# First attention: a pair's two early decay halves as one product of 128 columns, issued beside the late product

## What is computed

```python
g = -jax.nn.softplus(x @ Wg.T + bg)                 # (b, t, H), H = 8
lam = jax.nn.softplus(dl + Lparam[None, None])      # level weights
G = jnp.cumsum(g, axis=1)
scores = jnp.einsum('bthd,bshd->bhts', q, k) * scale
logdecay = Gh[:, :, :, None] - Gh[:, :, None, :]    # G[t] - G[s], Gh is G by heads
logdecay = jnp.where(mask[None, None], logdecay, -jnp.inf)
decay = jnp.exp(logdecay)
lamw = jnp.einsum('bthl,tsl->bhts', lam, lvl_oh)    # by the dyadic level of t - s
A = scores * decay * lamw
y = jnp.einsum('bhts,bshd->bthd', A, v)
```

## Time and profile before

| | |
|---|---|
| median of 3 runs | 1531.12 us (1529.8 to 1531.84) |
| profiled execution | 1537.38 us, span 1535.6 us |
| PE busy | 1417.6 us, 92% of the span |
| DVE, ACT, POOL busy | 920.9 (60%), 801.3 (52%), 660.2 us (43%) |
| chain that ended last | PE 68%, POOL 8%, DVE 7%, issue 6%, ACT 5%, DMA 3% |
| mean granted TensorE clock | 0.966 of full speed |

### The profile page before, as it was taken

How to read it: one execution, slowest core, us unless ns; L and a number is a source line. 1 busy time by engine, 2 the same in 40 slices (tenths; PEclk the granted TensorE clock), 3 DMA queues, 4 the chain that set the end, 5 groups by cost and what they waited for, 6 DMA issues and landing times.

```text
span 1535.6 us, 38290 instructions
## 1 busy us (share of the span) xinstructions
PE 1417.6 (92%) x14613; PEld 1068.8 (70%) x14613; DVE 920.9 (60%) x2370; ACT 801.3 (52%) x1526; POOL 660.2 (43%) x680
## 2 busy tenths in 40 slices
PE   6999999996999988998969998989999999998997
PEld 5666666665777756795646666767888888884864
DVE  3344444435888854541488999966676677756223
ACT  4544445444687754553446776755555555542531
POOL 3343445334235543003567777633333344443034
PEclk9999999998999988998979999999999999999999
DMA  5020330000375631138100000000000000001323
GB/s 159 17 63 24 83 113 8 12 1 5 143 285 183 228 125 56 48 99 300 49 11 7 2 2 2 2 14 1 6 6 8 13 11 9 7 13 37 104 69 87
DMA packets 97820, 92.60 MB, mean 60 GB/s; under 512 B 21869, under 2 KB 71658, under 8 KB 97386
## 3 DMA queue, kind: packets, MB, share of 16 engines
q1 hardware_dynamic: 93034, 80.71, 16.2%
q0 software_dynamic: 4608, 9.45, 2.0%
HBM read 31.92 MB, written 58.21 MB: 59 GB/s over the span
## 4 chain that ended last, share of the span: by engine, by line
PE 68%; POOL 8%; DVE 7%; issue 6%; ACT 5%; DMA 3%; SPq 1%; another core or an unknown queue 1%; POOLq 0%; DVEq 0%; ACTq 0%
PE bank L3201 6%; PE bank L1608 5%; PE bank L3236 5%; PE bank L1624 4%; PE bank L3215 4%; PE bank L3189 4%; PE bank L939 4%; PE bank L865 4%; PE bank L871 4%; POOL s_p L1287 3%; PE bank L895 3%; PE bank L916 3%; PE bank L3227 3%; PE bank L888 2%; PE bank L2575 2%
## 5 line engine op out<-in xcount | busy, mean ns | idle before, releaser
L1394 ACT COPY s_pT<-bank 77x512 f32<-77x512 f32 (+1 forms) x256 | 136.7, 584 | 93.0 <-PE bank L1608 90.1
L1608 PE MATMUL bank<-ident,s_p 128*77 128x128 f32 (+1 forms) x1024 | 149.2, 295 | 19.5 <-ACT s_p L1385 10.2
L2973 POOL TENSOR_TENSOR s_p<-s_p,s_inverse 128x616 f32<-128x616 f32 x64 | 77.0, 1223 | 204.6 <-DVE s_inverse L3116 204.6
L1608 PEld LDWEIGHTS bank<-ident,s_p 128*77 128x77 f32 (+1 forms) x1024 | 123.2, 155 | 50.9 <-ACT s_p L1385 28.8
L1287 POOL TENSOR_TENSOR s_p<-s_p,s_peak 128x1024 f32<-128x1024 f32 x64 | 120.2, 1900 | 33.6 <-DVE s_peak L1478 33.6
L1385 ACT ACTIVATE s_p<-s_p 128x616 f32<-128x616 f32 (+1 forms) x128 | 111.0, 887 | 29.5 <-POOL s_p L1287 25.7
L3100 DVE TENSOR_REDUCE s_peak<-bank 128x8 f32<-128x616 f32 x64 | 50.8, 794 | 96.6 <-PE bank L3215 95.0
L744 DVE TENSOR_TENSOR s_aT<-bank,s_weight 128x512 f32<-128x512 f32 (+1 forms) x64 | 44.2, 690 | 94.3 <-PE bank L916 58.1
L3201 PE MATMUL bank<-pos_bias,s_ctx 128*32 128x128 f32 x3072 | 90.9, 274 | 1.8 <-ACT s_kT L3011 1.7
L1464 DVE TENSOR_TENSOR s_p<-bank,pos_bias 128x1024 f32<-128x1024 f32 x64 | 77.7, 1218 | 21.8 <-PE bank L1597 21.8
L3031 ACT ACTIVATE s_p<-s_p 128x616 f32<-128x616 f32 x64 | 46.8, 732 | 83.7 <-DVE s_p L3104 83.7
(11 more groups left out here) (369 smaller groups left out, 3489.3 us busy)
## 6 DMA issues: line engine op xcount, KB each, us to landing
sorted_tokens<-s_zero SPq DMA_DIRECT2D x4, 5632.0 KB
sorted_tokens<-s_zero SPq DMA_DIRECT2D x8, 2560.0 KB, 13.5
routed_tokens<-s_routed SPq DMA_DIRECT2D x24, 256.0 KB, 2.4
s_tokens<-sorted_tokens SPq DMA_DIRECT2D x48, 64.0 KB, 1.8
s_rows<-sorted_tokens SPq DMA_DIRECT2D x48, 64.0 KB, 1.9
x_all<-x SPq DMA_DIRECT2D x8, 256.0 KB, 3.2
w_s_gateup<-s_gateup SPq DMA_DIRECT2D x1, 2048.0 KB
out<-x_all SPq DMA_DIRECT2D x8, 256.0 KB
```

What stands on the lines that cost most here:

```text
L1394: nc.scalar.copy(pT[0:keys, b % 2, 4 * q:4 * q + 4, :].rearrange("m h t -> m (h t)"), bank[0:keys, flip_bank("p", b, q), :]).then_inc(drai ...
L1608: last = nc.tensor.transpose(bank[0:keys, into, j * T:(j + 1) * T], p[:, b % 2, 4 * q + j, :], core.ident[:, :])
L2973: nc.gpsimd.tensor_tensor(part, part, inverse[:, b % 2, heads].unsqueeze(2).to_broadcast([P, HU, M]), ALU.mult).then_inc(share_ready, 1)
```

## The change

`stationary` for the early queries now holds the columns of the group's batches packed: partitions 0 to 63 have 4 x 64 columns side by side instead of 4 x 128 of which only the first 64 were read. The even and the odd batch of a pair thus have 128 columns next to each other, and the early unit becomes one product of 64 rows and 128 columns, of the same shape as the late unit's, which lies on the other 64 partitions. PE takes all its waits (the operands, the early unit's bank, the late unit's bank) ahead of the first product; before, the late bank was waited for between the two units. GpSimd's product for the early partitions writes 32x256 instead of 32x512. The constants have the same size as before.

```diff
@@ decay_constants
-    stationary = np.concatenate([chosen, 0 * chosen] * 2)
+    early = np.concatenate([np.repeat(of_batch, TH, axis=1), np.zeros((PAIR, G * TH), np.float32)], axis=1)
+    stationary = np.concatenate([early, 0 * chosen, chosen, 0 * chosen])
@@ stage1
+        def early_columns(g):
+
+            return stationary[:, g % 2, :, :].rearrange("p n t -> p (n t)")[:, 0:G * TH]
@@ operands_of (GpSimd)
                     rows = slice((2 * half + 1) * PAIR, (2 * half + 2) * PAIR)
+                    if half:
+                        columns, to = stationary[rows, g % 2, :, :], T
+                    else:
+                        columns, to = early_columns(g)[rows, :].rearrange("p (n t) -> p n t", t=TH), TH
                     nc.gpsimd.tensor_tensor(
-                        stationary[rows, g % 2, :, :], sums[rows, :].unsqueeze(1).to_broadcast([PAIR, G, T]),
-                        w.s1_of_batch[rows, :].unsqueeze(2).to_broadcast([PAIR, G, T]),
+                        columns, sums[rows, 0:to].unsqueeze(1).to_broadcast([PAIR, G, to]),
+                        w.s1_of_batch[rows, :].unsqueeze(2).to_broadcast([PAIR, G, to]),
                         ALU.mult).then_inc(operands_ready, 1)
@@ TensorE
-            def logdecay_of(u):
+            def logdecay_of(u, into):
                 b = batch_of(u)
                 g, n = b // G, b % G
-                pe.wait_ge(operands_ready, 4 * (g + 1))
-                into = fill("decay", u)
                 if is_early(u):
-                    rows = slice(0, 2 * PAIR)
-                    nc.tensor.matmul(bank[0:TH, into, :], stationary[rows, g % 2, n - 1, 0:TH], moving[rows, g % 2, :],
-                                     start=True, stop=True, tile_position=(0, 0))
-                    last = nc.tensor.matmul(bank[TH:T, into, :], stationary[rows, g % 2, n, 0:TH], moving[rows, g % 2, :],
-                                            start=True, stop=True, tile_position=(0, TH))
+                    rows, columns = slice(0, 2 * PAIR), early_columns(g)[0:2 * PAIR, (n - 1) * TH:(n + 1) * TH]
                 else:
-                    rows = slice(2 * PAIR, 4 * PAIR)
-                    last = nc.tensor.matmul(bank[:, into, :], stationary[rows, g % 2, n, :], moving[rows, g % 2, :],
-                                            start=True, stop=True, tile_position=(2 * PAIR, 0))
-                last.then_inc(filled, 1)
+                    rows, columns = slice(2 * PAIR, 4 * PAIR), stationary[2 * PAIR:4 * PAIR, g % 2, n, :]
+                nc.tensor.matmul(bank[:, into, :], columns, moving[rows, g % 2, :], start=True, stop=True,
+                                 tile_position=(rows.start, 0)).then_inc(filled, 1)
+
+            def logdecays_of(b):
+                pe.wait_ge(operands_ready, 4 * (b // G + 1))
+                banks = [(u, fill("decay", u)) for u in units_of(b)]
+                for u, into in banks:
+                    logdecay_of(u, into)
...
-                    for u in units_of(step):
-                        logdecay_of(u)
+                    logdecays_of(step)
```

## The result

The changed kernel took 1514.38 us (median of 4 runs, 1512.88 to 1515.88) against 1530.46 us for the kernel before on the same chip (4 runs, 1526.61 to 1531.84): a ratio of 0.9893 with a 95% interval of 0.9866 to 0.9920. Forecast were 1515.4 us and a range of 1512.5 to 1522.5. The profiled execution took 1515.03 us, its span 1513.2.

A forecast was written before the change was run, and what follows sets the result against it. PE was taken to bound the first attention. Products -16.0, moved wait +0.3 and GpSimd 0 gave -15.7 us, from the median of 1531.12 to 1515.4 us; range 1512.5 to 1522.5, chance of the forecast 0.80.

The forecast's parts named there:

- What bounds the stage: First attention, 30 to 344 us: PE busy 314.00 of 314 us, so time leaving PE there leaves the total.
- The products: Log-decay pairs of odd steps: early and late products overlap, 2.06 to 1.06 us a pair, 16 x 1.00 = 16.0 us saved.
- the nearest row's stagger: Between the starts of a pair's two products: 0.01 us, as L884 after L882, since L3171 starts its tiles as closely.
- The wider stagger of one L1597: Between a pair's products, the most a row shows: 0.25 us more, leaving 16 x 0.76 = 12.2 us saved.
- The strict turn: Rival at the pairs: passes go product by product, only the middle two overlap; pair 1.48 us, total 1522.1 us; chance 0.07.
- no overlap: Rival at the pairs: four passes run in turn; pair 1.91 us, 2.1 us saved, total 1529.0 us; chance 0.08.
- The wait moved forward: Late bank's wait ahead of the early product: +0.3 us, once, at step 11; nothing at step 23.
- The rival that it could cost more than the gain: At every pair PE meets the late bank's copy later, stalling 16 times: 1534.2 us or more; chance 0.03.
- What is late next: Engines feeding PE in the first attention: they lose only 1 us in about 21 per two steps; no further loss booked.
- the output product with its 1.67 us: Nearest deadline found, in an even step: its aT ends by 106.25, PE wants it at 107.92.
- GpSimd: One of two L519 products per group shrinks: between nothing and 8 x 0.52 = 4.1 us of POOL, 0 on the path.
- a microsecond or two for what follows the stage: After the first attention: the lower clock level may catch more or less PE work, a microsecond or two either way.

The follow-up runs named there:

- the run on the same rows: Changed kernel with every decay product on rows 0 to 63, the late log decay left out: pair 1.91 us, ratio 0.9989 to the kernel before.
- the two narrow products: Changed kernel with the early unit as two products of 64 columns again, waits ahead and columns packed: pair 2.06 us, ratio 1.0018 to the kernel before.
- the four quarters: Changed kernel with both units of odd steps as two products of 64 rows and 64 columns: pair 1.02 us, ratio 0.9875 to the kernel before.
- the later rounds: Changed kernel unaltered, measured again beside a version with the late bank's wait between the products: 1519.65 us, ratio 0.9888 to the kernel before.

## Why the prediction was right

*What bounds the stage.* PE did, and it still does; 1.00 us less a pair came out of the stage almost whole.

*The products.* Forecast 1.06 us a pair with the nearest row's stagger; measured 1.06. The wider stagger of one L1597 does not occur here. The strict turn (1.48) and no overlap (1.91) are excluded in the changed kernel; the price worked out for the second is what the run on the same rows measured, 1.91 us and 2.1 us of stage. The Trainium skill's rule on a change of the tiling mode ("TensorEngine Tiling (Array Packing)", Tiling Modes, Key Properties), which the rows before could not tell from a conflict of columns, agrees with the two narrow products and the four quarters: 2.06 us with two forms, 1.02 with one. A plain conflict of columns is excluded, since the changed pair shares all 128 of them; what the array does at a change of form no run shows beyond the late start.

*The wait moved forward.* Forecast 0.3 us, once, at step 11; the pair starts 0.32 us later there, of which the profile shows 0.2 as idle time, and step 23 shows no wait. The rival that it could cost more than the gain has nothing for it.

*What is late next.* This step failed in a small way. The nearest deadline was not the output product with its 1.67 us but GpSimd's level tile of step 1: 35.72 - 35.16 = 0.56 us to spare, less than the 1.00 us that PE gained ahead of it, so 0.48 us came back as a wait. The deadline came from where the steps repeat and not from the first ones, where GpSimd has just waited for VectorE. The sum for the stage is then 16.0 - 0.32 - 0.48 = 15.2 us, which is what was measured.

*GpSimd.* The narrower product took 604 ns, so 8 x (1036 - 604) = 3.5 us of POOL, within the bounds, and 0 on the path:

```profile
L528 POOL TENSOR_TENSOR s_chosen_rows<-s_sums,w_s_of_batch x16: 604/822/1040, 19.6 to 284.8; 32x256 f32<-32x256 f32 x8, 32x512 f32<-32x512 f32 x8
```

*The total.* The forecast was 15.7 us off the median, the first comparison gave 16.1, and the ratios of 0.9888 to 0.9893 mean 16 to 17 us. The trace vouches for 15.2. The microsecond or two between lies inside the intervals, and the middle stages, which vary by more, are enough for it; that it is theirs was not shown. The range was allowed a microsecond or two for what follows the stage, which was too little: one execution differs from the next by several there. So two nearnesses are partly luck, one good and one bad. The first median came within 1 us of the forecast; in the later rounds the changed kernel stood at 1519.65 us and the kernel before at 1535.48, and what held was their difference, 15.8 us. And the profiled execution was forecast at 1521.7 us and took 1515.03: of the 22.4 us between the two spans 15.1 are the stage, 8.0 the middle and 0.5 what lies ahead of the stage, and the rest gave 1.2 back.

## What to carry to other kernels

Where a few products share a place, give them all one tile shape and put them on different rows or columns of the array; what stands between a short product and its neighbour may be nothing but a change of shape. Read whether such tiles overlap from any other line of the same kernel that issues them in turn, and take the pair's time as that of one product. Before a saving on a saturated engine is booked in full, look for the tightest deadline at the stage's first steps too, and compare a stage's length in the trace when the change is near the spread of the total.

## What was not expected of the hardware

Quarters of the array in one form overlap as well as halves: eight passes of 64x64 tiles in 1.02 us, each pass with 512 columns, where L871 needs 0.43 us for one pass of 512 on the full array. And neither a met wait between two products (1.06 us) nor a semaphore raised by the first of them kept the second from starting beside it.

The middle of the program, with the first cross-attention and the first feed-forward part, took from 650.9 to 663.7 us in ten profiled executions. The long ones have the lower mean clock, as the table's runs show; what makes the clock fall for longer in one execution than in another stays open.
